# Two FFNs and an attention layer on one core: context blocks regrouped, idle products in the prologue, attention steps and weights moved

## What is computed

```python
gate_v, gate_o = top-2 of 8 sigmoids per row and head, normalised
q, k = x @ q_w[h], x @ k_w[h]                        # 8 heads of 128
v = sum_e gate_v[:, h, e] * (x @ v_w[h, e])
att = softmax(q k^T / sqrt(128)); ctx = att v
out = sum_h sum_e gate_o[:, h, e] * (ctx_h @ o_w[h, e])
```

## Time and profile before

| | us |
|---|---|
| median of 3 runs (1552.72 to 1558.23) | 1554.7 |
| the profiled execution | 1552.08 |
| its span, first to last instruction | 1550.3 |
| TensorE (PE) busy | 1469.3 (95%) |
| VectorE (DVE) busy | 1288.3 (83%) |
| ScalarE (ACT) busy | 1207.2 (78%) |
| GpSimd (POOL) busy | 978.7 (63%) |

### The profile page before, as it was taken

The page is one execution under the profiler, slowest core; times in us unless marked ns, Lnnn a source line. Parts: engine busy times, 40 slices in busy tenths (PEclk is TensorE's granted clock), DMA queues, the critical chain, the costliest instruction groups (busy, mean ns, idle before and its releaser), DMA issues. The chain is left out here.

```text
span 1550.3 us, 25823 instructions
## 1 busy us (share of the span) xinstructions
PE 1469.3 (95%) x7227; PEld 1099.2 (71%) x7227; DVE 1288.3 (83%) x3434; ACT 1207.2 (78%) x3587; POOL 978.7 (63%) x1719
## 2 busy tenths in 40 slices
PE   5899999999999999978888899999999999999997
PEld 3677788888888888743333357888888888888884
DVE  6889889888988877878888948988898889888874
ACT  3788888888888888737876787888888888888884
POOL 4578876777777777653241135777677767776665
PEclk8999999999999999999999999999999999999999
DMA  6234523333333335302211012333233323333321
GB/s 198 73 133 150 191 109 110 109 109 109 109 137 109 109 109 204 112 25 68 83 62 62 15 55 93 110 115 114 95 121 117 112 97 121 116 112 110 120 81 35
DMA packets 50837, 163.48 MB, mean 105 GB/s; under 512 B 3460, under 2 KB 26630, under 8 KB 34310
## 3 DMA queue, kind: packets, MB, share of 16 engines
q1 hardware_dynamic: 50694, 161.82, 29.9%
HBM read 136.64 MB, written 25.17 MB: 104 GB/s over the span
## 5 line engine op out<-in xcount | busy, mean ns | idle before, releaser
L992 ACT ACTIVATE vt<-bank,gate 128x128 f32<-128x128 f32 x1024 | 292.5, 371 | 168.4 <-PE bank L523 154.3
L1341 DVE SCALAR_TENSOR_TENSOR ot<-bank,gn,ot 128x128 f32<-128x128 f32 x1024 | 287.9, 343 | 80.2 <-ACT ot L1031 52.5
L1615 POOL TENSOR_TENSOR vt<-vt 128x256 f32<-128x256 f32 x256 | 198.7, 776 | 228.0 <-DVE vt L1327 227.8
L1031 ACT ACTIVATE ot<-bank,gn 128x128 f32<-128x128 f32 x1024 | 291.9, 370 | 40.9 <-PE bank L523 28.9
L1327 DVE SCALAR_TENSOR_TENSOR vt<-bank,gate,vt 128x128 f32<-128x128 f32 x1024 | 285.8, 341 | 12.3 <-ACT vt L992 9.4
L1640 POOL TENSOR_TENSOR ot<-ot 128x256 f32<-128x256 f32 x256 | 196.9, 769 | 101.6 <-DVE ot L1341 97.3
L1350 DVE TENSOR_TENSOR pt<-bank,pt 128x512 fp32r<-128x512 f32 x256 | 175.7, 686 | 78.3 <-ACT pt L1019 77.7
L521 PE MATMUL bank<-wv,xhl 128*128 128x512 f32 x512 | 223.3, 436 | 11.1 <-ACT vt L992 9.5
L521 PE MATMUL bank<-wo,chl 128*128 128x512 f32 x512 | 207.0, 404 | 18.3 <-DVE chl L1310 15.7
L1317 DVE TENSOR_REDUCE nmin<-bank 128x1 f32<-128x512 f32 x256 | 173.9, 679 | 45.8 <-PE bank L523 42.9
L522 PE MATMUL bank<-wo,chl 128*128 128x512 f32 x512 | 203.7, 398 | 0.0
(11 more groups left out here) (190 smaller groups left out, 3006.3 us busy)
## 6 DMA issues: line engine op xcount, KB each, us to landing
wv<-wv_split SPq DMA_DIRECT2D x56, 1024.0 KB, 4.9
wo<-wo_split SPq DMA_DIRECT2D x56, 1024.0 KB, 4.8
wv_split<-wv SPq DMA_DIRECT2D x8, 1024.0 KB, 5.0
wo_split<-wo SPq DMA_DIRECT2D x8, 1024.0 KB, 7.1
qk<-qk_rows SPq DMA_DIRECT2D x32, 256.0 KB, 2.9
qk_rows<-qs SPq DMA_DIRECT2D x24, 256.0 KB, 3.0
rawv<-in_L_ffn_v_w SPq DMA_DIRECT2D x8, 512.0 KB, 6.2
rawo<-in_L_ffn_o_w SPq DMA_DIRECT2D x8, 512.0 KB, 8.3
```

The source lines that it names most:

```text
L992: last = activation(vt[:, u % 2, e * P:(e + 1) * P], gb[0][:, e * P:(e + 1) * P], ACT.Copy, scale=gate[:, n % 2, k, h * E + e:h * E + e + 1])
L1031: last = activation(ot[:, u % 2, e * D:(e + 1) * D], gb[2][:, e * D:(e + 1) * D], ACT.Copy, scale=gn[:, j % 2, k, e:e + 1])
L1341: last = v.scalar_tensor_tensor(o, gb[3][:, e * D:(e + 1) * D], gn[:, j % 2, k, G + e:G + e + 1], o, ALU.mult, ALU.add)
L1615: own.link(g_.tensor_tensor(a[:, 0:2 * P], a[:, 0:2 * P], a[:, 2 * P:4 * P], ALU.add))
```

## The change

Constants: 36 idle products; context blocks by slot, none in slots 0 and 3, two each in slots 1 and 2; another division of the 30 attention steps beside slots 125 to 134. ScalarE's and VectorE's part of the context goes from the start of slot 0 of head g + 2 to the end of slot 2 of head g + 1. In the first FFN TensorE issues the idle products ahead of slot -2, after the set-up copies; they read `xhl` and `wv` and write `cb`, and nothing reads their result. In the attention layer `over_sum` goes from step 240 to 242, `weights` from 240 to 245, and the constant from step 10 of a batch to step 44.

```diff
--- before.py
+++ after.py
@@ -32,6 +32,8 @@
 STEPS = B * MU
 LAG = 30
 EARLY, LAST_SMALL = 6, 280
+IDLE_PRODUCTS = 36
+CONTEXT_BLOCKS = ((), (0, 1), (2, 3), ())
 CLEAR_SLOT, INPUT_SLOT = 72, 102
 PICKS = 12
 FIRST_PICKS = ((0, 3), (3, 6), (6, 8), (8, 10), (10, 12))
@@ -39,7 +41,7 @@
 FIRST_MHA, FIRST_AGAIN = B, 2 * B
 AGAIN, TURN_AGAIN, LOGITS_AGAIN, RANK_AGAIN = 160, 172, 178, 190
 STACK_HEADS = {26: ("stack", 0), 27: ("stack", 1), 28: ("constant", 0)}
-STEPS_BESIDE = {125: 2, 126: 2, 127: 2, 128: 4, 129: 4, 130: 4, 131: 3, 132: 3, 133: 3, 134: 3}
+STEPS_BESIDE = {125: 2, 126: 2, 127: 4, 128: 3, 129: 3, 130: 3, 131: 4, 132: 3, 133: 3, 134: 3}
 SLOTS_BEHIND = (260, 266, 272, 278, 290, 294, 298, 302)
 
 
@@ -723,9 +725,17 @@
                     split3(gb[2 + half][:], chl[:, j % 2, 0, c], chl[:, j % 2, 1, c],
                            wo[:, j % 2, 0, e, :], wo[:, j % 2, 1, e, :]).then_inc(done, 1)
 
+                def keep_clock():
+
+                    pe.wait_ge(setup_copied, 1)
+                    for _ in range(IDLE_PRODUCTS):
+                        mm(cb[:], xhl[0][:, 0, 0:P], wv[:, 0, 0, 0:G, :], start=True, stop=True)
+
                 def slot(t):
                     if t == -V_AHEAD:
                         query(0)
+                    if f == 0 and t == 1 - V_AHEAD:
+                        keep_clock()
                     g, k = t // QT, t % QT
                     j, n, h = head(g)
                     running = 0 <= t < TILES
@@ -751,8 +761,8 @@
                     if 0 <= t - O_BEHIND < TILES:
                         outputs(t - O_BEHIND, 0)
                         outputs(t - O_BEHIND, 1)
-                    if 1 <= g <= HEADS:
-                        context(g - 1, k)
+                    for c in CONTEXT_BLOCKS[k] if 1 <= g <= HEADS else ():
+                        context(g - 1, c)
 
                 return slot
 
@@ -1038,8 +1048,6 @@
                     g, k = t // QT, t % QT
                     _, n, h = head(g)
                     running = 0 <= t < TILES
-                    if k == 0 and 2 <= g < HEADS + 2:
-                        context(g - 2)
                     if t + V_AHEAD < TILES:
                         values(t + V_AHEAD)
                     if 0 <= t + V_AHEAD - 1 < TILES:
@@ -1070,6 +1078,8 @@
                         split_values(g + 2, halves[k - 1])
                     if 0 <= t - O_BEHIND < TILES:
                         outputs(t - O_BEHIND)
+                    if k == 2 and 1 <= g <= HEADS:
+                        context(g - 1)
 
                 return slot
 
@@ -1514,8 +1524,9 @@
                         own.then(v.reciprocal(xn[:, k, :], xn[:, k, :]))
                     if s >= RANK_AGAIN and (s - RANK_AGAIN) % 4 == 0 and s < RANK_AGAIN + 4 * PICKS:
                         pick_step((s - RANK_AGAIN) // 4)
-                    if s == RANK_AGAIN + 4 * PICKS + 2:
+                    if s == RANK_AGAIN + 4 * PICKS + 4:
                         over_sum(B)
+                    if s == RANK_AGAIN + 4 * PICKS + 7:
                         weights(B)
 
                 return step
@@ -1703,7 +1714,7 @@
                             stack_rest(at + 1, c)
                     if group_of(s, PUT_MAXIMA) is not None:
                         add_maxima(group_of(s, PUT_MAXIMA))
-                    if batch_of(s, 10) is not None:
+                    if batch_of(s, 44) is not None:
                         add_constant(b)
                     if b < B - 1 and r == 11:
                         rstd_(FIRST_MHA + b + 1)
```

## The result

The changed kernel takes **1542.4 us** (median of 4 runs, 1541.95 to 1542.61) against 1554.1 for the kernel before (4 runs, 1552.7 to 1558.2): a ratio of 0.9912, 95% interval [0.9886, 0.9937]. That is faster by more than 0.3%, inside the range, 1.4 us from the forecast. The profiled execution took 1542.5 us with a span of 1540.7, where the kernel before had 1550.3: 9.6 us less, and not the 13.5 of the sum.

A forecast was written before the change was run, and what follows sets the result against it. TensorE's own pace bounds the long FFN stretches, so only edges give time back (VectorE second bound there). Gains 4.0+4.0+1.0+2.3-1.0+0.75+2.5 = 13.55 take 1552.1 to 1538.5; plus 2.6 for the median, 1541 us, range 1532 to 1552.

The forecast's parts named there:

- signs of being right: Chl waits gone or under 2 us; no half clock at 21.8-32.1, 97, 879; slots 3.93/5.99/5.31/3.93; first gated matmul near 29.2.
- signs of being wrong: Waits for vt in many heads' slots 0/1; head over 19.2 us; idle products past 29 us; attention 702-890 no shorter.
- First heads: First FFN, 40 to 200 us: chl waits and half clock partly replaced by waits for values; 4.0 us gained (0 to 7.7).
- First FFN's tail: Chl waits at 663 and 683 us go, slot 128's outputs about half a us earlier; 4.0 us gained (0 to 9.8).
- Second FFN's start: Context block 0's 1.28 us wait for pt at 934 us goes, block one slot later; 1.0 us gained (0 to 1.3).
- The end: Waits at 1524 and 1535 us: first partly becomes a softmax wait, second goes; 2.3 us gained (0 to 3.6).
- Settled slots: VectorE's lag in two short slots, 1.3 us against 1.2 in hand, matters only with reciprocals; -1.0 us (0 to -22).
- the slow rival: Short slots 0 and 1 starve TensorE: 56 slots at 0.4 us each cost 22 us, 1562 in all; chance 0.10.
- Idle products: Before the first tile: 36 products fit the wait to 29.24 us and keep full clock; 0.75 us gained.
- Weights: Attention near 879 us: spreading over_sum and weights removes a 1.88 us wait and half clock; 2.5 us gained (0 to 5.3).
- The constant: Attention layer: POOL's addition 34 steps later, where POOL is idle; 0 us.
- The sum: Whole kernel: terms give 13.55 us, from the profiled 1552.1 to 1538.5; 2.6 added for the median gives 1541.

The follow-up runs named there:

- a2_old_context: Changed kernel with context blocks one per slot and copy and split at the start of slot 0 two heads on again: 1554.5 us, ratio 0.9994.
- a1: Changed kernel without the 36 idle products: 1547.1 us, ratio 0.9943.
- a4: Changed kernel with over_sum and weights back together in step 240: 1547.0 us, ratio 0.9939.
- b4: Changed kernel with 56 unused VectorE additions in slots 0 and 3 of heads 4 to 31 of the second FFN: 1550.2 us, ratio 0.9961.
- c4: Changed kernel with POOL's constant back in step 10 of each batch: 1540.6 us, ratio 0.9911.
- a3: Changed kernel with the old division of attention steps beside slots 125 to 134: 1539.6 us, ratio 0.9903.
- b2: Kernel before with only the context part of the change: 1545.6 us, ratio 0.9928.
- b3: Changed kernel with the old division of steps, over_sum spread over steps 241 to 244 and weights in step 246: 1539.6 us, ratio 0.9890.
- c1: b3 with four reciprocals four steps apart instead of two, and picks, sums and weights eight steps later: 1538.0 us, ratio 0.9888.
- c3: Changed kernel with 60 idle products in place of 36: 1546.9 us, ratio 0.9952.
- b1: Changed kernel with one context block per slot and copy and split at the end of slot 3 one head on: 1548.5 us, ratio 0.9945.
- c2: Changed kernel, unaltered, run and profiled again (its second execution): 1544.0 us over 10 runs, ratio 0.9929.

## Why the prediction was right, and where it was not

Of the prediction's signs of being right, the waits for chl, the clock at 22 to 32 and at 97 us and the pattern of the slots came; the one at 879 did not. Of its signs of being wrong one came: the attention layer got longer, by 2.6 us from step 32 to the second FFN's first values. Part by part:

- **First heads, 4.0 forecast.** 3.9 and 3.6 us measured, 0.1 the other way in a2_old_context. The step held: the 96 us wait and its half clock are gone, and smaller waits stand in their place. From 40 to 200 us those for the softmax on ScalarE rise from 2.7 us in two to 4.0 in four, those for the values on VectorE from 0.6 in three to 1.2 in seven. Forecast were the values alone.
- **First FFN's tail, 4.0.** 2.8 and 2.3 us. The wait for a maximum was foreseen. That slot 128's outputs come about half a us earlier held in the first execution (0.46, counted from tile 127's scores) and not in the second, nor in a1, a4, b4 and c4, where they come up to 0.12 us later than before; with the old division (a3, b2, b3, c1) they come 3.1 us earlier. So the size was off: I took the new division as harmless, and it costs 1.2 us (a3_old_steps).
- **Second FFN's start, 1.0.** 2.0 us, above the bound of 1.3: the wait for pt of 1.28 us is gone; the other 0.7 is the context part's too (a2_old_context has none of it), but I have no row for its cause.
- **The end, 2.3.** 2.0 us.
- **Settled slots, -1.0.** Nothing measurable. Scores of four tiles, timeline of the changed kernel:
```profile
1106.20 0.40 PE L523 MATMUL bank<-xhl,qhl 128*128 128x512 f32 x1
...
1111.51 0.39 PE L523 MATMUL bank<-xhl,qhl 128*128 128x512 f32 x1
...
1115.42 0.39 PE L523 MATMUL bank<-xhl,qhl 128*128 128x512 f32 x1
...
1119.35 0.39 PE L523 MATMUL bank<-xhl,qhl 128*128 128x512 f32 x1
```
  The slots of 5.31, 3.91 and 3.93 us are the forecast's. VectorE's lead over TensorE fell from 1.90 to a median of 1.16 us in the short slots, as worked out (1.2), and to 0.48 at the least: the reciprocals do not use it up. b4_vector_load shows that the slow rival's 0.4 us for each of 56 busy slots was too high by four times.
- **Idle products, 0.75.** 0.7 us by the same stretch in both kernels, 1.35 against a1 and b2; what is left of it at tile 28 is not shown. They ran at full clock, 0.23 us apart. The 0.9 us by which the changed kernel's first gated values start earlier are not theirs: the second execution has 0.1 of it. The Trainium skill ("TensorE: Matmul & The Clock Gate", Part 1) has it that activity releases the throttle, that is, lets the clock up. Here the trace agrees: the clock was 1.00 from 12.9 to 50.4 us with the products, and 0.50 from 24.3 to 34.5 without.
- **Weights, 2.5 (0 to 5.3): this step failed;** 1.8 us were lost. It had two halves. The wait of 1.88 us goes, as forecast: 1.94 us from step 240 to 244. But I took the half clock behind it as its consequence, to be gone with it, and it doubled to 13.7 us: 3.75 us lost up to the second FFN. a4_old_weights loses the same with the wait in place, so the clock there does not follow this wait. b3, c1, c4 and a1 have full clock at that place, and a1 changes nothing in the attention layer.
- **The constant, 0.** No difference at its own place (steps 64 to 128: 0.02 us against c4), and at most some 0.3 us in the tail; what the clock did in c4 is not shown to be its work.

**The sum.** By landmarks the parts gave 9.5 us, not 13.5; of the 4.0 missing, the weights stretch is 4.3, the attention ahead of it 0.8, the tail 1.2 and three smaller ones 0.7, against 1.0 more from the second FFN's start, 1.1 from the settled slots and 0.9 from the prologue. The median met the forecast closer than that because the profile of before lay 2.6 us under the median that I added back, while that of the changed kernel lies at its own. The reason is the clock, of which the sum knows only the stretches in that one profile: before was profiled at 0.984, as good as the best of its 52 other executions, and has 0.980 on average, the changed kernel 0.985. The 1.4 us of the median are thus luck in good part; the 4 us of the sum are the true miss.

**What stays open** is what sets the clock in the attention layer. The stretch of half clock that begins at or soon behind step 244 has these lengths in the profiles:

| kernel | half clock, us |
|---|---|
| changed kernel (both), b4 | 13.7 |
| a3, c3 | 17.1 |
| a2, b1 | 3.4 |
| a1 | 0 |
| old weights: before, a4, b2 | 6.8, 17.1, 3.4 |
| c4, b3, c1 | 0 |

The first eight profiles have one and the same program for the attention layer behind its first 30 steps, and span the whole range from 0 to 17.1 us. So neither the weights nor the constant nor the order of those steps decides it. Untested is how much of it one kernel shows from execution to execution: only the changed kernel has two profiles, and they agree here. I have no rule by which it could have been forecast. b3_spread, a3_old_steps and c1_spread_more have the lowest medians, 1539.6, 1539.6 and 1538.0 us. The ratios of b3 and c1, 0.9890 [0.9869, 0.9911] and 0.9888 [0.9858, 0.9918], touch that of the changed kernel, so that they beat it is likely, by the 1.2 us of the old division that all three have, but not settled by the times.

## What to carry to other kernels

A split or copy that another engine waits for belongs ahead of the work that has slack, and the bank it reads must be finished early enough: moving only its place in the queue brought 3.3 of 11.2 us at the edges, 1.8 of 7.7 in all. A part that only comes along with a change (here a new division of steps, 1.2 us lost in a gain of 4) should be tried without it. Where a gain is smaller than the scatter of runs, compare the traces product by product, and profile the same kernel more than once to learn what such a difference is worth. And set the mean granted clock beside every time: here it explains most of the scatter, and a profile taken at an unusually good clock (0.984 against 0.980) made the kernel before look 4 us faster than it is on average. A wait that is seen ahead of a half-clock stretch need not be its cause.

## What the runs showed of the hardware that was not expected

- In attention, with products of 32 rows, the granted clock was 0.50 for stretches of 3.4 to 17.1 us while TensorE was shown busy for over 90% of most of them (12.65 of 13.70 us at 873.1). Kernels with the same attention layer had between 0 and 17.1 us of it at the same place (a1_no_idle and c3_idle_60); the two profiles of the changed kernel had 13.7 us both.
- The mean granted clock of unchanged kernels ran from 0.975 to 0.984 (before, 52 executions) and from 0.980 to 0.988 (c2, 10 executions), and the spans with it from 1561.5 to 1548.0 and from 1546.9 to 1537.3 us: about 1 us for each 0.001.
- 36 products that nobody reads held the clock at 1.00 through a wait of 9.5 us without delaying the product behind it (28.3 and 29.1 us against 29.2); 24 more, past the end of the wait, cost 4.3 to 5.1 us at that place.
- Two executions of one kernel drifted by 1.3 us over 500 us of settled slots (0.27%), with clock 1.00 in both.
